# A router that reads unnormed rows, a new order of events in the recurrence, and expert loops written out on VectorE

## The reference

```
x2 = layernorm(x1 + moe0(x1))                # eps 1e-5
r  = x2 + recurrence(x2)                     # its own layernorm inside, gamma, beta, eps 1e-5
x3 = layernorm(x2 + r)                       # = layernorm(2*x2 + y @ Wo + bo)
logits = x3 @ router_w                       # 14 columns; argmax and softmax over them
out = layernorm(x3 + moe1(x3))
```

## Time and profile before

| | |
|---|---|
| median of 3 runs | 628.72 us (626.07 to 634.33) |
| the profiled execution's own time | 618.04 us |
| its span | 616.2 us |
| busy: PE, DVE, ACT, POOL | 467.1 (76%), 357.4 (58%), 257.1 (42%), 275.5 (45%) |
| mean granted clock of PE | 0.892 of full |

### The profile page before, as it was taken

One profiled execution on the slowest core, in us unless ns is written; L12 is line 12 of the kernel. 1 busy time (PEld: TensorE's weight loads), 2 busy tenths in 40 slices (PEclk: granted clock), 3 DMA queues, 4 the chain that ended last, 5 costly groups with the idle time before them and its releaser, 6 DMA issues.

```text
span 616.2 us, 10401 instructions
## 1 busy us (share of the span) xinstructions
PE 467.1 (76%) x3099; PEld 324.2 (53%) x3099; DVE 357.4 (58%) x868; ACT 257.1 (42%) x502; POOL 275.5 (45%) x324
## 2 busy tenths in 40 slices
PE   4888999999999999997669991787692955377710
PEld 3465665656666666564349981335261634266610
DVE  2467666677767776771435554776554252455545
ACT  1055567656665667672115450654231111133300
POOL 3342563367545733402136664342526243267741
PEclk9989999999999999996679997899796877599975
DMA  9999999999970000003011215400000000112222
GB/s 325 174 173 171 229 277 168 169 173 162 164 108 2 1 6 14 1 1 119 12 43 45 59 44 178 189 2 0 2 0 17 14 4 18 37 52 74 54 69 68
DMA packets 69386, 52.58 MB, mean 85 GB/s; under 512 B 3238, under 2 KB 67501, under 8 KB 68704
## 3 DMA queue, kind: packets, MB, share of 16 engines
q1 hardware_dynamic: 66592, 47.83, 42.2%
q0 software_dynamic: 2752, 4.23, 2.2%
HBM read 21.41 MB, written 32.06 MB: 87 GB/s over the span
## 4 chain that ended last, share of the span: by engine, by line
PE 14%; issue 11%; POOL 9%; DVE 9%; DMA 4%; ACT 1%; SPq 1%; DVEq 1%; POOLq 0%; ACTq 0%
PE banks L967 4%; POOL returned L609 3%; PE banks L976 3%; DVE xc L1393 2%; POOL regions L518 2%; PE banks L1034 1%; DMA returned<-work,back 1%; DVE sta L1376 1%; PE banks L1023 1%; POOL arena L656 1%; DVE xb L1385 1%; DMA xa<-returned 1%; PE banks L959 1%; PE banks L1045 1%; PE banks L1014 1%
## 5 line engine op out<-in xcount | busy, mean ns | idle before, releaser
L682 ACT ACTIVATE arena<-banks 128x512 f32<-128x512 f32 x128 | 76.4, 597 | 88.5 <-PE banks L849 88.2
L849 PE MATMUL banks<-ca,work 128*128 128x128 f32 x512 | 83.2, 286 | 18.7 <-ACT arena L682 16.0
L675 ACT ACTIVATE work<-banks,nmax 128x512 f32<-128x512 f32 x128 | 80.7, 686 | 16.4 <-DVE nmax L1221 16.2
L849 PEld LDWEIGHTS banks<-ca,work 128*128 128x128 f32 x512 | 54.3, 142 | 55.6 <-issue 44.2
L721 ACT ACTIVATE work<-banks,arena 128x128 f32<-128x128 f32 x156 | 46.1, 366 | 81.2 <-PE banks L967 81.2
L1221 DVE TENSOR_REDUCE nmax<-banks 128x2 f32<-128x1024 f32 x64 | 78.4, 1224 | 2.2
L609 POOL DMA_INDIRECT returned<-work,back x54 | 62.8, 1162 | 34.9 <-POOL back L604 16.8
L833 PE MATMUL banks<-arena 32*128 32x512 f32 (+3 forms) x256 | 60.6, 438 | 0.0
L822 PEld LDWEIGHTS banks<-arena 32*128 32x128 f32 x256 | 41.7, 186 | 31.5 <-issue 25.6
L822 PE MATMUL banks<-arena 32*128 32x128 f32 x256 | 55.8, 298 | 1.3 <-DVE corr L1304 0.7
L1340 DVE COPY arena<-arena 128x642 f32 (+1 forms) x54 | 33.3, 617 | 35.4 <-DVE work L1353 32.3
(11 more groups left out here) (193 smaller groups left out, 795.9 us busy)
## 6 DMA issues: line engine op xcount, KB each, us to landing
regions<-zeros SPq DMA_DIRECT2D x24, 1032.0 KB, 20.8
arena<-wp_in SPq DMA_DIRECT2D x1, 4624.0 KB, 26.6
arena<-wp_in SPq DMA_DIRECT2D x1, 4494.0 KB, 15.1
arena<-regions SPq DMA_DIRECT2D x54, 64.5 KB, 1.8
arena<-ct_in SPq DMA_DIRECT2D x1, 2048.0 KB, 10.0
xa<-returned SPq DMA_DIRECT2D x8, 256.0 KB, 3.8
arena<-cb_in SPq DMA_DIRECT2D x1, 1667.0 KB, 8.3
ca<-ca_in SPq DMA_DIRECT2D x1, 1098.0 KB, 5.6
```

Of the source, the lines that this page charges most:

```text
L675: eng.activation(prob[:, r, :], bank[r], ACT.Exp, bias=nmax[:, s % 2, jj:jj + 1]).then_inc(s_exp, 1)
L682: eng.activation(probT[:, v % 2, j0 + jj, :, i % 2 * P:(i % 2 + 1) * P], PT.rearrange("p (t q) -> p t q", t=TB), ACT.Copy).then_inc(s_pTs, 1)
L849: mm = eng.transpose(PT[:, t * P:(t + 1) * P], prob[:, 2 * (s % 2) + jj, t * P:(t + 1) * P], ident)
```

## The change

1. **Loops.** DVE's expert loop is written out slot by slot in both stages. The waits and ring places are constants, and the offset of slot m+1 is loaded into its register right after the copy of slot m's weights instead of just before its own copy.
2. **Rows.** x2 is no longer made: the four events `normed` are gone (16 DVE instructions). POOL makes twice the reciprocal deviation instead of once (constants 0.25), and `out b` is four DVE instructions of 128 columns, xc times that per row plus bank 7. The row's mean stays in, and the next norm takes it out.
3. **Router.** One DVE instruction makes a centring matrix, one PE product and one ACT copy make centred router weights (event `mean`, in bank 7). PE's `router b` transposes the unnormed rows xc right after `out`; it no longer waits for x3. A new event `scale b` on DVE multiplies the picked logits by the rows' deviations before the softmax; the softmax waits for it. POOL's second scatter waits for x3.
4. **Table.** One small Sigmoid is put ahead of the recurrence on ACT.
5. **Order.** The list of events is another.

```
 def plan_recurrence():
-        ("sum", 0), ("sum", 1), ("z", 0), ("turn", 0), ("in", 0), ("normed", 0), ("z", 1), ("turn", 1), ("sum", 2),
-        ("conv", 0), ("sc", 0), ("sg", 0), ("in", 1), ("u", 0), ("z", 2), ("turn", 2), ("conv", 1), ("sc", 1), ("sg", 1),
-        ("gate", 0, 0), ("normed", 1), ("u", 1), ("sum", 3), ("gate", 0, 1), ("scan", 0, 0), ("normed", 2), ("z", 3),
-        ("in", 2), ("sg", 2), ("scan", 0, 1), ("turn", 3), ("conv", 2), ("gate", 1, 0), ("sc", 2), ("u", 2), ("out", 0),
-        ("gate", 1, 1), ("scan", 1, 0), ("x3", 0), ("router", 0), ("normed", 3), ("in", 3), ("sg", 3), ("conv", 3),
-        ("scan", 1, 1), ("logits", 0), ("gate", 2, 0), ("sc", 3), ("u", 3), ("rank", 0), ("scatter", 0), ("out", 1),
-        ("gate", 2, 1), ("scan", 2, 0), ("x3", 1), ("router", 1), ("scan", 2, 1), ("logits", 1), ("gate", 3, 0),
-        ("rank", 1), ("scatter", 1), ("out", 2), ("gate", 3, 1), ("scan", 3, 0), ("x3", 2), ("router", 2),
-        ("scan", 3, 1), ("logits", 2), ("rank", 2), ("out", 3), ("scatter", 2), ("x3", 3), ("router", 3), ("logits", 3),
-        ("rank", 3), ("scatter", 3)]
+        ("mean", 1), ("sum", 0), ("sum", 1), ("z", 0), ("turn", 0), ("in", 0), ("sum", 2), ("z", 1), ("sg", 0), ("turn", 1),
+        ("conv", 0), ("sc", 0), ("in", 1), ("u", 0), ("sg", 1), ("z", 2), ("conv", 1), ("gate", 0, 0), ("turn", 2),
+        ("sc", 1), ("u", 1), ("sum", 3), ("scan", 0, 0), ("gate", 0, 1), ("z", 3), ("scan", 0, 1), ("gate", 1, 0),
+        ("in", 2), ("sg", 2), ("conv", 2), ("scan", 1, 0), ("out", 0), ("sc", 2), ("u", 2), ("turn", 3), ("gate", 1, 1),
+        ("router", 0), ("scan", 1, 1), ("in", 3), ("sg", 3), ("x3", 0), ("conv", 3), ("gate", 2, 0), ("logits", 0),
+        ("sc", 3), ("u", 3), ("scale", 0), ("scan", 2, 0), ("out", 1), ("rank", 0), ("gate", 2, 1), ("scan", 2, 1),
+        ("scatter", 0), ("x3", 1), ("router", 1), ("gate", 3, 0), ("logits", 1), ("scale", 1), ("scan", 3, 0), ("out", 2),
+        ("rank", 1), ("gate", 3, 1), ("x3", 2), ("scan", 3, 1), ("scatter", 1), ("router", 2), ("logits", 2),
+        ("scale", 2), ("out", 3), ("rank", 2), ("router", 3), ("x3", 3), ("scatter", 2), ("logits", 3), ("rank", 3),
+        ("scale", 3), ("scatter", 3)]
 ...
 # POOL
+                if l:
+                    eng.wait_ge(s_x3, TB * (b + 1))                      # in scatter
-                eng.tensor_scalar(rstda[:, 0, tiles], mva[:, 0, tiles, 1], 1.0, 1e-5, ALU.mult, ALU.add).then_inc(s_gstep, 1)
+                eng.tensor_scalar(rstda[:, 0, tiles], mva[:, 0, tiles, 1], 0.25, 0.25e-5, ALU.mult, ALU.add)\
+                   .then_inc(s_gstep, 1)
 ...
 # ACT
-                eng.wait_ge(s_pick[l], B)                                # in router_exp
+                eng.wait_ge(*((s_pick[0], B), (s_scaled, B))[l])
+            eng.activation(few[:, 0:1], half[:, 0:1], ACT.Sigmoid).then_inc(s_outa, 1)
+                if kind == "mean":
+                    eng.wait_ge(s_mean, 1)
+                    eng.activation(rw[:, :], bank[7][:, 0:E1], ACT.Copy).then_inc(s_rw, 1)
 ...
 # PE
+                if kind == "mean":
+                    eng.wait_ge(s_cr, 16)
+                    eng.wait_ge(s_cen, 1)
+                    eng.matmul(bank[7][:, 0:E1], cen[:, :], R("router"), start=True, stop=True).then_inc(s_mean, 1)
                 elif kind == "router":
-                    eng.wait_ge(s_x3, TB * (b + 1))
+                    eng.wait_ge(s_res, TB * (b + 1))
-                        mm = eng.transpose(bank[6][:, t * P:(t + 1) * P], xb[:, b * TB + t, :], ident)
+                        mm = eng.transpose(bank[6][:, t * P:(t + 1) * P], xc[:, b * TB + t, :], ident)
                 elif kind == "logits":
-                        mm = eng.matmul(..., xnT2[:, t * P:(t + 1) * P], R("router"), ...)
+                        mm = eng.matmul(..., xnT2[:, t * P:(t + 1) * P], rw[:, :], ...)
 ...
 # DVE
-                def fetch(m, r, first):
-                    off = eng.value_load(offs[0:1, bass.ds(m, 1)], ...)
-                    if not first:
+                def place(m):
+                    return eng.value_load(offs[0:1, m:m + 1], ...)
+                def fetch(m, r, off):
+                    if m >= RING:
                         eng.wait_ge(s_y[l], m - (RING - 1))
                         eng.wait_ge(s_yb[l], m - (RING - 1))
                     eng.tensor_copy(wbuf[:, r, 0:width], wp[:, bass.ds(off, width)]).then_inc(s_wb[l], 1)
-                for m in range(2 * RING):
-                    fetch(m, m % RING, m < RING)
+                off = place(0)
+                for m in range(nt):
+                    fetch(m, m % RING, off)
+                    if m + 1 < nt:
+                        off = place(m + 1)
                     turned(m, m % RING, m < RING)
                     if m >= 2:
                         result(m - 2, (m - 2) % RING, (m - 2) // RING, m - 2 < RING)
-                with eng.Fori(2, nt // RING) as it:
-                    ...
+            eng.scalar_tensor_tensor(out=cen[:, :], in0=C("ones"), scalar=-1.0 / D, in1=A("ident"), op0=ALU.mult, op1=ALU.add)\
+               .then_inc(count(s_cen), 1)
-                elif kind == "normed":
-                    ...
                 elif kind == "out":
-                    eng.scalar_tensor_tensor(out=xb[:, b * TB:(b + 1) * TB, :], in0=xb[...], scalar=2.0, in1=bank[7]...)
-                    stats_of(xb, 0, tiles)
+                    for t in tiles:
+                        eng.scalar_tensor_tensor(out=xc[:, t, :], in0=xc[:, t, :], scalar=rstda[:, 0, t:t + 1],
+                                                 in1=bank[7][:, (t - b * TB) * P:(t - b * TB + 1) * P],
+                                                 op0=ALU.mult, op1=ALU.add).then_inc(count(s_res), 1)
+                    stats_of(xc, 0, tiles)
+                elif kind == "scale":
+                    eng.wait_ge(s_pow, npow + place_of[(0, "out", b)])
+                    own()
+                    part = by_tile(lg[:, b * TB * E1:(b + 1) * TB * E1], E1)
+                    eng.tensor_tensor(part, part, over_e(rstda[:, 0, b * TB:(b + 1) * TB], E1), ALU.mult)\
+                       .then_inc(count(s_scaled), 1)
```

More of the change, by code:

```diff
@@ L389, in build @@
         s_cwb = sem("s_cwb")
+        s_cen = sem("s_cen")
+        s_mean = sem("s_mean")
+        s_rw = sem("s_rw")
+        s_scaled = sem("s_scaled")
         s_turn = sem("s_turn")
@@ L1362, in experts @@
                         result(m - 2, (m - 2) % RING, (m - 2) // RING, m - 2 < RING)
-                with eng.Fori(2, nt // RING) as it:
-                    for r in range(RING):
-                        fetch(it * RING + r, r, False)
-                        turned(it * RING + r, r, False)
-                        result(it * RING + (r - 2), (r - 2) % RING, it if r == 2 else it - 1, False)
                 for m in range(nt - 2, nt):
```

21 lines of the change are left out of this document (10 added, 11 removed).

## The result

The changed kernel takes 594.39 us (median of 4 runs, 588.18 to 597.82), the kernel before 627.39 beside it (4 runs, 620.69 to 634.33). The ratio is 0.9475, with a 95% interval of 0.9339 to 0.9611: about 33 us, or 5%, faster. The profiled execution took 588.18 us, with a span of 586.3, 1.9 less.

The account below looks back on a forecast made before the run. The first expert stage was taken as near PE's limit, the recurrence as bound by engines waiting for each other. Savings 5.0 + 2.4 + 27.3 = 34.7 from 618.0 gave 583.3; plus 10.7, 594.0 us, range 580 to 612.

Parts of the forecast that it names:

- The recurrence, 27.3: Recurrence: new router and order win 27.3 us, 31.3 count less 4; ends 18 and 34.
- The walk: Recurrence: new event list followed, engine by engine, at traced durations; scatter 3 at 495.3 instead of 526.6, 31.3 us.
- the deduction of 4: Recurrence: 4 us taken off for some 80 hand-overs at up to 0.05 and PE's clock after its holes.
- the signs named for a wrong forecast: Late turned with 2.2 us slots; 3 us x3 on over three sequences' chain; recurrence clock under 0.8; u 3 ending after 455.
- First expert stage, 5.0: First expert stage: 1.93 us a slot against 2.21 over 18 loop slots wins 5.0 us; ends 0 and 5.6.
- The ring closes at about 1.9 us as well: First expert stage: the path through POOL's store and SP's load is late next, at about 1.9 us a slot.
- The cover of the fetch copy's new place: Expert loops: DVE's earlier copy ends only 0.08 us past the start of POOL's store; counted as nothing.
- Second expert stage, 2.4: Second expert stage: eight loop turns, each no longer delaying a result by 0.3 us, win 2.4; ends 0 and 5.
- Half of it: Recurrence: the router's hole turns into holes before rank and u, so 19 us won, 609.7; chance 0.15.
- More: Second stage's ring shortens fully, PE's clock stays high, products don't slow DVE: 584 to 580 us; chance 0.10.
- No change: Loops win nothing because the register load takes as long, and order wins under 12 us: 620; chance 0.07.
- Slower: PE's clock stays at the lower level in recurrence and first expert stage: 656 us; chance 0.04.

Follow-up runs that it names:

- experiments 1 to 4: Parts apart, ratios to the kernel before: written-out loops alone 0.9916; changed kernel with old order 0.9637, with old router and no early table load 0.9726, with old loops 0.9517.
- all_out: Changed kernel with the expert loops of SP, PE and ACT written out too, SP's register loaded early; 584.3 us, ratio 0.937 to the kernel before.
- new_router_old_order: Changed kernel keeping the old list of events, with mean in front and scale behind each rank; 606.32 us, ratio 0.9637 to the kernel before.
- experiments 7, 9 and 12: Changed kernel with all expert loops written out, 584.3 us; that with six loaded-row buffers, 588.43; that plus gate 1,1 earlier and row-number copies on ACT, 580.79.
- after: The changed kernel itself, with the whole change, against the kernel before; 594.39 us, ratio 0.9475.

## Why the prediction was right

The forecast was 594.0, the median is 594.39. So close a hit is luck. The recurrence won 3.1 us more than forecast and the expert stages 4.0 less. And for the profiled execution 583.3 was forecast and 588.18 came, 4.9 more, 4.1 of them from attention, which the change doesn't touch; but the median stood 6.2 us above it and not the 10.7 that the sum took over from the kernel before, which gave 4.5 back.

- **What bounds it.** Right. The recurrence's hole ahead of the router was the price of x3's place, and experiments 1 to 4 show it from both sides: with the router still on x3, PE waits 9.09 us for it in the new list too.
- **The recurrence, 27.3; measured 30.4.** The walk had 31.3, before 4.0 were taken off for hand-overs and the clock. Its marks, counted from the first sum (379.25 before, 380.70 after), held: out 0 at 43.45 (measured 43.29), out 1 64.35 (65.89), router 1 78.15 (79.94), out 3 100.05 (101.33), scatter 3 116.05 (116.96). In this trace the deduction of 4 was the mis-sized term. All the hops of the walk, for whose 0.05 us each no row was given, and the slow out 0 (7.2 us at a granted clock of 0.62, where 4.5 was put down) cost 0.9 us on balance. How that balance splits isn't measured, but one of the walk's own numbers erred the other way: x3 took 2.07 to 2.09 us. The 3.05 of the earlier trace rows had been read as x3 beside one POOL product, and it was x3 beside two. Gate 3,0 took 6.36 us where 5.3 was put down. Over the six traces of this recurrence the gain is 27.4 to 30.4, so that 27.3 is just below them, and a deduction of 0.9 to 3.9 would have been right.
- **PE's wait ahead of router 1, 3.4 by DVE's read of rank 0.** Measured 3.74, by that read. Of the signs named for a wrong forecast none came: u 3 ended 74.5 us after the first sum, where the limit of 455 is 75.75. From the last expert result to the second stage's first load, "about 130 instead of 160": 504.44 - 374.69 = 129.75 against 533.42 - 373.17 = 160.25.
- **First expert stage, 5.0; measured 2.7 (about 4 over all traces).** The rate was nearly right: 1.93 us a slot forecast, 1.9 to 2.05 in most, 5.97 for three. One hole of 1.9 us for a landing took most of the missing 2.3. "The ring closes at about 1.9 us as well" had named the loads as late next, but the hole comes once and not in every kernel, and what makes it isn't shown; `all_out` is 2.2 us shorter without it. The gap of "about 0.1" is 0.20. No run leaves the load out, so how much of the 0.20 is the load's stays open.
- **The cover of the fetch copy's new place.** Counted as nothing. The copy ends 0.19 us behind the store's start instead of the forecast 0.08, and POOL's store fell all the same, from a mean of 1.28 to 1.04 us in the first stage, since the late copies of before overlapped it more. That this shortened the stage isn't shown.
- **Second expert stage, 2.4; measured 0.8.** Even the 0.8 isn't told from nothing: with DVE's loops written out and nothing else changed in this stage, four other traces took 64.99 to 66.69 us and `new_router_old_order` 72.36, against 65.20 before. The term that failed is the prediction's 8 x 0.3, for a result that the loop's end delays eight times. It took the ring of loads for the only limit. POOL (1.52 us a slot when it never waits) and DVE (1.41 to 1.53) are each within 0.3 of the 1.6 to 1.7 that a slot takes, so whatever is freed of one is lost at the next: experiments 7, 9 and 12 opened one after the other, and none of them brought this stage below after's 64.4 by more than 0.1.
- **Rivals.** *Half of it* had its mechanism right in part (router 3 does wait 2.47 us for the read of rank 2, router 1 3.74), but not its size. *More* wanted 5 us from the second stage's ring, which gave 0.8 at most; of its other two conditions the clock did rise, from 0.81 to 0.88, and x3 was slowed less. *No change* wanted under 12 us from the order; order and router together won 30. *Slower* needed the lower level throughout; the first stage kept 0.95.
- **The table load, 1.28.** It is gone from the path in the rows; no run could tell its worth.

## What to carry to other kernels

When a product waits for a normed operand, ask whether the norm can be moved behind the product; but move the order too, since the freed engine stops at the next thing that was queued late (15 and 11 us apart, 27 to 30 together). A list walked, with each operation at its duration in the trace, gave every mark within 1.8 us over 117 us; what it leaves out and what it overstates may cancel, so a flat deduction needs a row behind it. In a loop where several queues are within a few tenths of a microsecond of one another, no single relief shows: add up each queue's time per slot first. And when an operation is slow in a trace, count what ran beside it: 3.05 us was the price of two neighbours, not of one.

## What the runs showed of the hardware

- With a register load directly before it, DVE's weight copy started 0.52 us behind the operation ahead; with the load one operation earlier, 0.20.
- POOL's indirect store takes 0.98 us alone, and is longer by the time for which a DVE copy within SBUF still runs at its start, less some 0.13: 1.04, 1.17, 1.36 and 1.45 us at 0.19, 0.32, 0.50 and 0.60.
- POOL's and DVE's work hold each other up in unequal amounts: POOL's copy of 128 numbers takes 0.18 to 0.21 us alone and up to 0.50 beside DVE's weight copy; DVE's x3 1.12 alone, 2.09 beside one POOL product and 3.05 beside two; and a scan of only 70 columns 1.95 instead of 0.30:

```profile
470.03 1.95 DVE L1138 TENSOR_TENSOR_SCAN upto_tile<-run,own 128x70 f32<-128x70 f32 x1
...
482.63 0.30 DVE L1138 TENSOR_TENSOR_SCAN upto_tile<-run,own 128x70 f32<-128x70 f32 x1
```

  The first runs beside POOL's product at 470.54 to 471.81, the second beside an indirect store and is no longer than with nothing beside it (0.30 at 448.17).
- Around a wait of 3.54 us PE's clock fell, and out 0 took 7.2 us instead of 4.5; after waits of 0.86 and 0.87 us in two kernels out 3 was slow in one (6.2 us) and not in the other (4.6).
- The same recurrence took 116.96 to 119.98 us in six traces, so single profiles tell no step under some 2 us there.
